# Talking-heads top-k attention on one core: the missed-row test moved to GpSimd, the pick placed inside the guess update, and one value copy moved from ScalarE to VectorE

## The reference

```python
dots = einsum('bhij,hk->bkij', einsum('bhid,bhjd->bhij', q, k) * scale, pre_proj)
dots = where(causal, neg, dots)
vk = lax.top_k(dots, 64)[0][..., -1:]
dots = where(dots < vk, neg, dots)
attn = einsum('bhij,hk->bkij', softmax(dots), post_proj)
out = einsum('bhij,bhjd->bhid', attn, v)
x = x + layernorm(out @ Wo + bo)
x = x + layernorm(ffn(layernorm(x)))
```

## Time and profile before

| | |
|---|---|
| Median of 3 runs (least, greatest) | 3318.77 us (3317.39, 3321.68) |
| The profiled execution | 3324.22 us, span 3322.4 us, mean TensorE clock 0.954 |
| VectorE busy | 2884.4 us, 87% |
| ScalarE busy | 2882.6 us, 87% |
| TensorE busy (matmul) | 2794.6 us, 84% |
| GpSimd busy | 1737.9 us, 52% |
| DMA | 22.93 MB, 1.7% of the engines' time for the program's own queue |

### The profile page before, as it was taken

The page is one execution under the profiler, slowest core; times in us unless marked ns, Lnnn a source line. Parts: engine busy times, 40 slices in busy tenths (PEclk is TensorE's granted clock), DMA queues, the critical chain, the costliest instruction groups (busy, mean ns, idle before and its releaser), DMA issues. The chain is left out here.

```text
span 3322.4 us, 76028 instructions
## 1 busy us (share of the span) xinstructions
PE 2794.6 (84%) x16314; PEld 2046.5 (62%) x16314; DVE 2884.4 (87%) x12547; ACT 2882.6 (87%) x8666; POOL 1737.9 (52%) x3623
## 2 busy tenths in 40 slices
PE   6888888888878888888898878888788898888865
PEld 3466666666656666666666656666566666666654
DVE  4599888989989899998889989989889889998884
ACT  1699899998978989899898979989899898989972
POOL 3355555555545555555555545545555555555543
PEclk9999999999989999999999989999999999999987
DMA  1000000000000000000000000000000000000000
GB/s 45 7 2 2 5 8 5 9 2 5 9 5 9 2 12 2 5 9 5 9 2 12 2 5 8 2 12 2 5 9 5 9 2 12 2 5 9 2 8 4
DMA packets 31421, 22.93 MB, mean 7 GB/s; under 512 B 3201, under 2 KB 30338, under 8 KB 30722
## 3 DMA queue, kind: packets, MB, share of 16 engines
q1 hardware_dynamic: 30722, 16.03, 1.7%
HBM read 11.83 MB, written 4.19 MB: 5 GB/s over the span
## 5 line engine op out<-in xcount | busy, mean ns | idle before, releaser
L915 ACT ACTIVATE signs<-scores,state 128x528 int8<-128x528 f32 (+3 forms) x3072 | 1726.3, 585 | 40.5 <-DVE state L1148 40.0
L784 PE MATMUL t_bank<-diag,probs 128*128 128x128 f32 x5120 | 760.9, 308 | 453.8 <-POOL diag L1349 400.5
L1349 POOL TENSOR_SCALAR diag<-ident,rinv 128x128 f32<-128x128 f32 x1024 | 362.2, 374 | 1360.1 <-DVE rinv L1195 1360.1
L784 PEld LDWEIGHTS t_bank<-diag,probs 128*128 128x128 f32 x5120 | 694.2, 216 | 494.1 <-issue 359.1
L1357 POOL TENSOR_TENSOR work<-scores,work 128x528 f32<-128x528 f32 (+3 forms) x1024 | 889.0, 903 | 10.8 <-DVE work L1075 10.8
L760 PE MATMUL s_bank<-xn,gT 128*128 128x512 f32 (+3 forms) x2048 | 685.7, 457 | 0.9 <-ACT gT L846 0.7
L771 PEld LDWEIGHTS y_bank<-u_all,probsT 128*128 128x128 f32 x5120 | 609.0, 192 | 107.3 <-issue 98.9
L915 ACT ACTIVATION_READ_ACCUMULATOR signs<-scores,state 128x1 f32 x3072 | 646.5, 210 | 0.0
L926 ACT COPY probsT<-t_bank 128x512 f32<-128x512 f32 (+1 forms) x768 | 406.9, 530 | 266.3 <-PE t_bank L784 265.1
L771 PE MATMUL y_bank<-u_all,probsT 128*128 128x128 f32 x5120 | 617.3, 276 | 5.3 <-ACT probsT L926 5.3
L1075 DVE TENSOR_SCALAR_CACHE_REDUCE work<-scores,state 128x528 f32<-128x528 f32 (+3 forms) x1024 | 531.1, 553 | 46.2 <-DVE state L1148 46.2
(11 more groups left out here) (156 smaller groups left out, 2846.5 us busy)
## 6 DMA issues: line engine op xcount, KB each, us to landing
xwork<-in_L_attn_x_dram SPq DMA_DIRECT2D x17, 256.0 KB, 2.8
xres<-in_L_attn_x_dram SPq DMA_DIRECT2D x16, 256.0 KB, 2.9
out_dram<-ybuf SPq DMA_DIRECT2D x16, 256.0 KB, 2.4
u_all<-in_L_attn_Wq_dram SPq DMA_DIRECT2D x1, 512.0 KB, 3.6
u_all<-in_L_attn_Wk_dram SPq DMA_DIRECT2D x1, 512.0 KB, 4.5
u_all<-in_L_attn_Wv_dram SPq DMA_DIRECT2D x1, 512.0 KB, 5.5
u_all<-in_L_attn_Wo_dram SPq DMA_DIRECT2D x1, 512.0 KB
expo<-in_L_ffn_w_gate_dram SPq DMA_DIRECT2D x1, 192.0 KB, 4.7
```

Source lines behind the costliest of these rows:

```text
L784: mm = nc.tensor.matmul(t_bank[q % 2][:, at:at + P], lhsT=probs[:, h % 2, KEY_AT[t] + j * P:KEY_AT[t] + (j + 1) * P], rhs=diag[:, t, :], s ...
L915: nc.scalar.activation(signs[:, k, AT[t]:AT[t] + ROW[t]], row(scores, ring(head_of(s, k + 1), RING), t), ACT.Sign, bias=guesses(s % STATES ...
L1349: nc.gpsimd.tensor_scalar(diag[:, t, :], ident[:, :], rinv[:, slot_p, t:t + 1], 1.0, ALU.mult, ALU.mult).then_inc(scaled, 1)
```

## The change

1. Ranks, spread and missed become three GpSimd operations that stand between the diagonals and the hiding operations, one step earlier than the test stood before. `offset` gets two halves and two more columns per tile, the count's distance from both ends of the allowed window; their product is positive where the row is missed.
2. `between` of the guess update, a difference of two old states, is made by GpSimd a step ahead, and VectorE waits for it.
3. The pick is split: its product (`weigh_ranks`) stands between the last two operations of the guess update, its sum (`pick`) behind it.
4. TensorE makes the flag right behind the scores; VectorE sums the four flags while it copies them.
5. The first extra of a step, where it is a U, is copied by VectorE at the end of its step.
6. In steps 11 to 13 the second feed-forward product stands behind one more count.

```diff
@@ tensor
             score(kind, b, par, s, g)
+        if lagged(kind, s, LAG_E):
+            raise_flag(kind, g - LAG_E, head_of(s, LAG_E) % 2)
         make_extra(kind, b, par, s, 0)
...
-        if lagged(kind, s, LAG_E):
-            raise_flag(kind, g - LAG_E)
@@ scalar
         elif use[0] == "U":
-            take_values(kind, b, par, use[1])
+            if place == 1:
+                take_values(kind, b, par, use[1])
@@ vector
-        v.tensor_copy(flags[:, :], flag_part).then_inc(flag_taken, 1)
+        v.tensor_scalar(flags[:, 0:T], flag_part, 1.0, None, ALU.mult, ALU.add,
+                        accum_out=flags[:, T:T + 1]).then_inc(flag_taken, 1)
...
-    dve.wait_ge(offset_ready, gp + 1)
-    dve.wait_ge(select_step, T + 1)
-    v.scalar_tensor_tensor(out=offset[:, :, 0:9], in0=offset[:, :, 0:9], scalar=0.0,
-                           in1=candidates(past), op0=ALU.is_equal, op1=ALU.mult)
-    v.tensor_reduce(kth[...], offset[:, :, :], AX_X, ALU.add).then_inc(kth_ready, 1)
-if checks:
-    v.scalar_tensor_tensor(out=spread[:, :], in0=number, scalar=-2.0 * AIM, in1=number, ...)
-    v.scalar_tensor_tensor(out=missed[:, 0:T], in0=spread[:, :], ..., in1=active, ...)
...
-    v.tensor_tensor(between[:, :, :], pair(past, S_T, -1), pair(last, S_OTHER, 0), ALU.subtract)
...
-    dve.wait_ge(guess_step, 3)
+    dve.wait_ge(guess_step, 2)
+    dve.wait_ge(between_ready, g - 1)
+    alone(dve)
...
     dve.sem_clear(guess_step)
+    if applies:
+        weigh_ranks()
     v.tensor_tensor(guesses(now, 1, GUESSES), guess, move[:, :], ALU.subtract).then_inc(guess_ready, 1)
+if applies:
+    if not moves:
+        weigh_ranks()
+    pick()
...
+use = extra(kind, s, 0)
+if use is not None and use[0] == "U":
+    dve.wait_ge(misc_full, misc_index(kind, b, use) + 1)
+    at_least(dve, pv_done, (b - 1) * H + 4 * (u // 4) + 4)
+    alone(dve)
+    v.tensor_copy(u_all[:, u % 4, 512 * (u // 4):512 * (u // 4 + 1)], misc[...][:, :])
@@ gpsimd
-    if lagged(kind, s, LAG_E):
-        nc.gpsimd.tensor_tensor(offset[:, :, 0:9], ranks, found[:, (s - 1) % 2, :]..., ALU.add)
     extras(kind, b, s)
+    if moves_next:
+        at_least(pool, guess_ready, g - 1)
+        nc.gpsimd.tensor_tensor(between[:, :, :], pair((s - 1) % STATES, S_T, -1),
+                                pair(s % STATES, S_OTHER, 0), ALU.subtract).then_inc(between_ready, 1)
...
     if lagged(kind, s, LAG_K):
+        at_least(pool, kth_ready, gk - 1)
+        pool.wait_ge(found_ready, 4 * gk + 4)
+        nc.gpsimd.tensor_tensor(ranked[:, :, 0:11], ranks, found[:, s % 2, :]..., ALU.add)
+        pool.wait_ge(offset_ready, gk + 1)
+        nc.gpsimd.tensor_tensor(spread[:, :], ranked[:, :, 0:1]..., ranked[:, :, 1:2]..., ALU.mult)
+        pool.wait_ge(spread_ready, gk + 1)
+        at_least(pool, flag_full, gk - 1)
+        nc.gpsimd.tensor_scalar(missed[:, slot_k % 2, :], spread[:, :], 0.0, 1.0, ALU.is_gt, ALU.mult)
         for p, t in enumerate(ORDER):
             pool.wait_ge(found_ready, 4 * gk + p + 1)
```

More of the change, by code:

```diff
@@ L343, in build @@
         found = sb("found", [P, 2, T])
-        offset = sb("offset", [P, T, 10])
+        offset = sb("offset", [P, 2, T, 12])
         spread = sb("spread", [P, T])
-        missed = sb("missed", [P, T + 1])
+        missed = sb("missed", [P, 2, T])
         flags = sb("flags", [1, T + 1])
@@ L444, in build @@
         select_step = sem("select_step")
+        spread_ready = sem("spread_ready")
         bad_ready = sem("bad_ready")
@@ L748, in raise_flag @@
                     pe.wait_ge(masked, 4 * H * B)
-                nc.tensor.matmul(flag_part, lhsT=onesP[:, 0:1], rhs=missed[:, :], start=True, stop=True,
+                nc.tensor.matmul(flag_part, lhsT=onesP[:, 0:1], rhs=missed[:, par_e, :], start=True, stop=True,
                                  skip_group_check=True).then_inc(flag_full, 1)
@@ L1055, in _ @@
             dve.wait_ge(state_set, 3)
-            nc.vector.tensor_copy(offset[:, :, 9:10].squeeze(2), cap)
+            nc.vector.tensor_copy(offset[:, :, :, 11:12].squeeze(3), cap.unsqueeze(1).to_broadcast([P, 2, T]))
             def batch(kind, b, par):
@@ L1077, in count_found, with weigh_ranks, pick @@
                                         accum_out=found[:, s % 2, t:t + 1]).then_inc(found_ready, 1)
+                    def weigh_ranks():
+                        dve.wait_ge(offset_ready, gp + 1)
+                        dve.wait_ge(select_step, T)
+                        v.scalar_tensor_tensor(out=offset[:, slot_p % 2, :, 2:11], in0=offset[:, slot_p % 2, :, 2:11], scalar=0.0,
+                                               in1=candidates(past), op0=ALU.is_equal,
+                                               op1=ALU.mult).then_inc(select_step, 1)
+                    def pick():
+                        dve.wait_ge(select_step, T + 1)
+                        dve.sem_clear(select_step)
+                        v.tensor_reduce(kth[:, bass.ds(slot_p, 1), :].squeeze(1), offset[:, slot_p % 2, :, 2:12], AX_X,
+                                        ALU.add).then_inc(kth_ready, 1)
                     if applies:
@@ L1122, in step @@
                         v.tensor_tensor(miss, counts[:, (s - 1) % 2, :], aim_sum, ALU.subtract).then_inc(guess_step, 1)
-                        v.tensor_tensor(between[:, :, :], pair(past, S_T, -1), pair(last, S_OTHER, 0),
-                                        ALU.subtract).then_inc(guess_step, 1)
                         dve.wait_ge(guess_step, 1)
@@ L1166, in step @@
                                                ).then_inc(misc_free[gate_at], 1)
+                    if selects:
+                        count_found(ORDER[1])
+                    if 11 <= s < 11 + HC and kind != "first":
                         dve.wait_ge(misc_free[gate_at], turns_of_bank(kind, b, misc_at(kind, ("GATE", c))) + 1)
@@ L1333, in step @@
                                               head_mem(smem[par], s)).then_inc(mem_placed, 1)
-                    if lagged(kind, s, LAG_E):
-                        at_least(pool, kth_ready, g - LAG_E)
-                        pool.wait_ge(found_ready, 4 * (g - LAG_E) + 4)
+                    extras(kind, b, s)
+                    moves_next = any(lagged(kind, s + 1, k + 2) for k in range(GUESSES)) if s + 1 < H else kind != "drain"
+                    if moves_next:
+                        at_least(pool, guess_ready, g - 1)
+                        at_least(pool, first_ready, g if kind != "drain" or s == 0 else 0)
                         alone(pool)
-                        nc.gpsimd.tensor_tensor(offset[:, :, 0:9], ranks,
-                                                found[:, (s - 1) % 2, :].unsqueeze(2).to_broadcast([P, T, 9]),
-                                                ALU.add).then_inc(offset_ready, 1)
-                    extras(kind, b, s)
+                        nc.gpsimd.tensor_tensor(between[:, :, :], pair((s - 1) % STATES, S_T, -1), pair(s % STATES, S_OTHER, 0),
+                                                ALU.subtract).then_inc(between_ready, 1)
                     gp, slot_p = g - LAG_P, head_of(s, LAG_P) % 2
@@ L1352, in step @@
                         gk, slot_k = g - LAG_K, ring(head_of(s, LAG_K), RING)
+                        ranked = offset[:, slot_k % 2, :, :]
+                        at_least(pool, kth_ready, gk - 1)
+                        pool.wait_ge(found_ready, 4 * gk + 4)
+                        alone(pool)
+                        nc.gpsimd.tensor_tensor(ranked[:, :, 0:11], ranks,
+                                                found[:, s % 2, :].unsqueeze(2).to_broadcast([P, T, 11]),
+                                                ALU.add).then_inc(offset_ready, 1)
+                        pool.wait_ge(offset_ready, gk + 1)
+                        alone(pool)
+                        nc.gpsimd.tensor_tensor(spread[:, :], ranked[:, :, 0:1].squeeze(2), ranked[:, :, 1:2].squeeze(2),
+                                                ALU.mult).then_inc(spread_ready, 1)
+                        pool.wait_ge(spread_ready, gk + 1)
+                        at_least(pool, flag_full, gk - 1)
+                        alone(pool)
+                        nc.gpsimd.tensor_scalar(missed[:, slot_k % 2, :], spread[:, :], 0.0, 1.0, ALU.is_gt,
+                                                ALU.mult).then_inc(bad_ready, 1)
                         for p, t in enumerate(ORDER):
```

53 lines of the change are left out of this document (20 added, 33 removed).

## The result

The changed kernel takes 3341.08 us (median of the runs) where the kernel before takes 3321.38 beside it: ratio 1.0065, 95% interval 1.0049 to 1.0081. It is slower, by 20 us. One of its five executions took 9865.03 us, at a mean granted clock of 0.469; it is not in the ratio, no trace of it was kept, and its cause is open. The profiled execution ran 3345.65 us, with a span of 3343.7.

The account below looks back on a forecast made before the run. VectorE was taken as the bound. The terms summed to +1.5 us per batch, +24 for 16 batches: 3348 us profiled, 3342 against the median, less 2 for the first batch: 3340, range 3235 to 3390, likeliest case 3295 to 3375.

Parts of the forecast that it names:

- the collision: VectorE's guess update, now earlier, waits for GpSimd's hiding operations, since two-input SBUF operations lock each other out; chance 0.50.
- GpSimd's three operations cost 1.0: Ranks, spread and missed delay hiding by 1.0 us, counted from R, the start of VectorE's reciprocal of the row sums.
- The plain step: Step without copy or statistics: the guess update meets hiding operations two to four, step 0.47 us longer, four per batch.
- The step with a copy: Steps with a value copy on VectorE and no statistics: 0.54 us longer, seven per batch.
- Behind statistics: Steps 7, 8, 14, normalisation statistics ahead of MAX8: 0.43 us shorter; steps 0 and 10, with a copy too, -0.2 each.
- The flag: VectorE's wait for TensorE's flag in step 7 goes, as it comes right behind the scores: -1.3 us per batch.
- Long GpSimd operations: Stretched L1148 of steps 1, 9, 15 escapes GpSimd's normalisation; probs operations take two of the hits: net -0.4 us per batch.
- L1170 loses its gap, -0.6: VectorE's L1170 gets a count ahead of it and loses its 0.20 us gap, three times: -0.6 us per batch.
- Half a collision: Rival: GpSimd's three operations cost nearer 0.4 than 1.0, the chain rides one seam earlier: 3190 to 3290 us; chance 0.25.
- The chain loses a seam: Rival: between hiding operations GpSimd's next goes first, 0.5 us more in 9 steps: +72 us more, 3400; chance 0.13.
- No collision: Rival: the guess update slips between GpSimd's accesses and the free sum holds, -10.5 us per batch: 3151 us; chance 0.07.
- ScalarE or TensorE as the bound: Rival: ScalarE or TensorE sets the pace in place of VectorE, then about 3350 us; chance 0.05.

Follow-up runs that it names:

- e3: The changed kernel with TensorE's flag again behind the G product: 3348.34 us, ratio 1.0080 to the kernel before.
- e2: The changed kernel with all value copies back on ScalarE: 3381.01 us, ratio 1.0179 to the kernel before.
- e4: The changed kernel with GpSimd's hiding cut to 16 columns per tile and the row maximum as softmax threshold: 3161.65 us, ratio 0.9512 to the kernel before.
- e5: The changed kernel with GpSimd's tests behind pmem and two small tiles hidden a step later: 3171.45 us, ratio 0.9548 to the kernel before.
- run 170: Not a run's label: "run" is a verb here, in "e4 and e5 ... run 170 to 180 us faster".

## Why the prediction was right, and where two errors cancelled

It forecast 3340 us by the collision, and 3341.08 was measured. Point by point:

- *GpSimd's three operations cost 1.0* and shift hiding to R+2.8: R+2.81.
- *The plain step.* First operation to end at 5.15, second at 5.88, third at 6.33, L1138 (now L1135) at 6.58: 5.14, 5.88, 6.33 and 6.49. Step 6: +0.50, predicted +0.47.
- *The step with a copy*: +0.54 predicted, steps 2 to 5 +0.43, +0.58, +0.54, +0.57. The copy's 0.60 from L1170: 0.61 from L1228 to MAX8.
- *Behind statistics*: step 14 -0.53, predicted -0.43; step 7 with the flag -1.77, predicted -1.73. Step 0 -0.31 and 10 -0.03, predicted -0.2 each. Step 8 -0.12, predicted -0.43: probs operations in it take 0.6 us of stretch more than before, which the term for long GpSimd operations holds.
- *The flag*: its wait is gone. e3 shows that the reason given, the early matmul, is a third of it; the rest is not shown, most likely the test a step ahead.
- *Long GpSimd operations*: L1148's 2.7 us of stretch per batch are gone (the prediction knew of 2.3 in steps 1, 9 and 15 and missed 0.4 in step 8), and in three steps, where I said two, a probs operation takes the hit. GpSimd's timeline of the changed kernel in step 8:

```profile
1544.84 1.04 POOL L1285 TENSOR_TENSOR ybuf<-ybuf,rstd 128x512 f32<-128x512 f32 x1
1546.01 0.73 POOL L1291 TENSOR_TENSOR xres<-xres,ybuf 128x256 f32<-128x256 f32 x1
1546.69 1.19 POOL L1292 TENSOR_TENSOR xres<-xres,ybuf 128x256 f32<-128x256 f32 x1
```

and VectorE's, where two probs operations of 0.76 and 0.63 us take 1.28 and 1.08:

```profile
1546.02 1.28 DVE L1196 SCALAR_TENSOR_TENSOR probs<-scores,kth,expo 128x528 f32<-128x528 f32 x1
1547.23 1.08 DVE L1196 SCALAR_TENSOR_TENSOR probs<-scores,kth,expo 128x400 f32<-128x400 f32 x1
```

  It comes to 2.6 us against 3.0 before (the probs operations of step 8 had 0.3 already): -0.4, as predicted.
- *L1170 loses its gap, -0.6*: mis-sized. The two feed-forward products take 4.34 us per batch where they took 4.54, since the second (L1179) is now followed by gaps of 0.15 to 0.4, and step 12 grew by 0.68 in place of 0.27.
- *What the sum had no term for*: the kernel before held 1.3 us per batch of gaps at fixed places, 21 us in all, and the changed kernel happens to have none. Taken out on both sides, the change costs about 2.7 us per batch and not 1.5. Steps 11 to 13 cost 0.6 more than their terms (L1170's 0.4 is in it), step 10 0.2, step 1 0.1, and the small wait's 0.2 did not show; with rounding that is the difference.

So the mechanism and its moments were right, and that the total fell within 2 us is partly luck: about 20 us of unpriced gain met about 20 us of cost that was too small. The range of 3235 to 3390 was wider than the moments needed. *Half a collision* falls with GpSimd's measured 1.0. *The chain loses a seam* did not happen in the changed kernel; in e2 the first operation starts earlier and waits for the end of the same operation, it is not passed over. *No collision* gives the time of e4 to 10 us, once its cause is removed. *ScalarE or TensorE as the bound* falls too: e4 and e5 leave both their work and run 170 to 180 us faster.
The Trainium skill (SBUF — State Buffer, Who interferes with whom) has two-input VectorE operations and GpSimd's locked out for whole instructions; e4 agrees, with 696 ns against 184, and all VectorE operations that stretched by more than 0.1 us have two SBUF inputs, while counts, MAX8 and the emptying of scores kept their times to 0.02 us beside the same GpSimd work.

## What to carry to other kernels

Before small two-input VectorE operations are moved forward, mark GpSimd's long operations from the event that releases them and see in which one each of the small ones would start: the gain is whatever the wait for its end leaves, and work added to GpSimd ahead of that point costs the whole chain. Short work that nobody waits for goes behind GpSimd's long operations, not ahead of them (126 us here, by order alone). And under one per cent, compare versions with their code shifted too: 64 fills that do nothing moved four kernels by 8 to 24 us.

## What I had not expected of the hardware

- VectorE stalls 0.2 to 1.0 us at fixed places of its instruction stream, the same every second batch. They were 0.05 to 3 us per batch of 196 and moved when the code did. The cause stays open.
- An operation freed 0.6 earlier waited 0.6 longer (L1118 of e2, 747 ns against 208): beside a locked resource the moment of the release is fixed by the other engine, and the added copies of 0.60 us cost 6 to 18 us in all in place of 86.
- GpSimd's small operations hold VectorE too: beside pmem, negmax and the memory scores (0.2 to 0.3 us each) L1131, L1135 and L1137 take 0.32, 0.24 and 0.27, where they take 0.16 to 0.18 in e4, and each ends within 0.04 us of one of them.
- The wait goes both ways. GpSimd's two operations L1291 and L1292, 256 columns each, take 0.73 us in e4; in the changed kernel most of them take 1.05 to 1.28, as the 1.19 of L1292 in step 8 above, beside VectorE's long probs operations.
